# Sixteen heads: values and ones in one stationary tile, with halves exchanged by a shuffle

## What is computed

```python
def _mha(xq, xk, xv, Wq, bq, Wk, bk, Wv, bv, Wo, bo, causal):
    ...
    s = jnp.einsum('bhqe,bhke->bhqk', q, k) * (1.0 / math.sqrt(D_MODEL))
    ...
    w = jax.nn.softmax(s, axis=-1)
    o = jnp.einsum('bhqk,bhke->bhqe', w, v)
    ...
    return o @ Wo.T + bo
```

## Time and profile before

| what | us |
|---|---|
| median of 3 runs | 1870.6 |
| lowest and highest run | 1862.0, 1876.38 |
| the profiled execution | 1865.85 |
| its span (first to last instruction) | 1864.1 |
| PE busy in it | 1732.8 |
| DVE, ACT, POOL busy | 763.1, 650.5, 133.3 |

### The profile page before, as it was taken

How to read it: one execution, slowest core, us unless ns; L and a number is a source line. 1 busy time by engine, 2 the same in 40 slices (tenths; PEclk the granted TensorE clock), 3 DMA queues, 4 the chain that set the end, 5 groups by cost and what they waited for, 6 DMA issues and landing times.

```text
span 1864.1 us, 36432 instructions
## 1 busy us (share of the span) xinstructions
PE 1732.8 (93%) x16204; PEld 1128.2 (61%) x16204; DVE 763.1 (41%) x1644; ACT 650.5 (35%) x1257; POOL 133.3 (7%) x318
## 2 busy tenths in 40 slices
PE   7999989999999998999999999999899889868998
PEld 6555546656566555555567775554577666654565
DVE  1344445454553224431123332324466666652222
ACT  2343434343544343211133331225333333313333
POOL 1111010000000000000000000000011111110000
PEclk9888999999998999899999999999799999979999
DMA  3211000000000001000010000000000000001022
GB/s 136 87 42 33 17 24 2 2 2 2 2 2 2 23 0 69 1 19 1 0 69 1 2 2 23 0 1 6 23 2 2 2 2 2 2 26 42 1 60 71
DMA packets 19214, 37.45 MB, mean 20 GB/s; under 512 B 2001, under 2 KB 17137, under 8 KB 17777
## 3 DMA queue, kind: packets, MB, share of 16 engines
q1 hardware_dynamic: 19056, 35.12, 5.6%
HBM read 33.48 MB, written 1.64 MB: 19 GB/s over the span
## 4 chain that ended last, share of the span: by engine, by line
PE 85%; DVE 11%; ACT 2%; issue 1%; DMA 0%; SPq 0%; DVEq 0%; ACTq 0%
PE psum L389 37%; PE psum L525 10%; PE psum L702 9%; PE psum L434 7%; PE psum L505 7%; DVE maxima L1279 3%; PE psum L502 2%; PE psum L472 2%; DVE denoms L1306 2%; PE psum L793 2%; PE psum L821 1%; PE psum L834 1%; PE psum L790 1%; PE psum L802 1%; DVE t L1368 1%
## 5 line engine op out<-in xcount | busy, mean ns | idle before, releaser
L1279 DVE TENSOR_REDUCE maxima<-psum 100x2 f32<-100x722 f32 (+3 forms) x332 | 249.6, 761 | 240.8 <-PE psum L472 129.9
L389 PE MATMUL psum<-x_resid,weights 128*128 128x400 f32 x832 | 294.7, 504 | 3.5 <-ACT q_then_o L914 1.3
L974 ACT ACTIVATE probs<-psum 128x800 f32<-128x800 f32 (+3 forms) x240 | 179.0, 748 | 296.4 <-PE psum L505 295.6
L389 PEld LDWEIGHTS psum<-x_resid,weights 128*128 128x128 f32 x832 | 156.1, 191 | 119.5 <-issue 3.4
L702 PE MATMUL psum<-weights 128*128 128x400 f32 x512 | 175.0, 499 | 0.7 <-DVE maxima L1279 0.7
L434 PE MATMUL psum<-ctx_t,weights 128*128 128x361 f32 x384 | 148.6, 517 | 27.9 <-DVE maxima L1279 26.7
L389 PE MATMUL psum<-weights,ctx_t 128*128 128x256 f32 (+1 forms) x576 | 162.8, 409 | 0.7 <-ACT weights L914 0.7
L502 PE MATMUL psum<-max_rows,ones_bf 32*128 32x100 bf16 (+7 forms) x1152 | 137.5, 236 | 19.4 <-DVE max_rows L1290 12.7
L957 ACT ACTIVATE values<-psum 128x256 f32<-128x256 f32 (+2 forms) x176 | 67.4, 383 | 218.6 <-PE psum L389 218.5
L702 PEld LDWEIGHTS psum<-weights 128*128 128x128 f32 x512 | 97.2, 190 | 75.1 <-DVE maxima L1279 0.8
L1306 DVE RECIPROCAL denoms<-psum 128x200 f32<-128x200 f32 x65 | 91.4, 1406 | 107.5 <-PE psum L525 107.5
(11 more groups left out here) (144 smaller groups left out, 2214.8 us busy)
## 6 DMA issues: line engine op xcount, KB each, us to landing
weights<-in_w SPq DMA_DIRECT2D x2, 3072.0 KB, 10.3
staged<-in_ctx SPq DMA_DIRECT2D x32, 128.0 KB, 2.1
values<-in_ctx SPq DMA_DIRECT2D x32, 128.0 KB, 2.2
weights<-in_w SPq DMA_DIRECT2D x3, 1024.0 KB, 4.8
weights<-in_src SPq DMA_DIRECT2D x1, 2368.0 KB, 13.6
weights<-in_w SPq DMA_DIRECT2D x1, 2048.0 KB, 8.8
weights<-in_tw SPq DMA_DIRECT2D x2, 1024.0 KB, 5.1
staged<-in_ctx SPq DMA_DIRECT2D x16, 105.0 KB, 2.1
```

The lines of the kernel that those rows point to most:

```text
L389: i = nc.tensor.matmul(PS[0:rows, bk, 0:n], lhs, rhs, start=k == 0, stop=k == len(terms) - 1)
L974: nc.scalar.activation(PT[0:kn, k % PROBS_KEPT, :, 0:n], PS[0:kn, bk:bk + 2, 0:n], ACT.Exp).then_inc(act_results, mark("act", f"{t} p{b} { ...
L1279: nc.vector.reduce_max(top, src, AX).then_inc(dve_results, mark("dve", f"{t} m{b} {j}"))
```

## The change

The zeros in `values` become ones, so the stationary tile of e = 0 is [values | ones] and that of e = 1 is [ones | values]. The two products go to two places in the bank instead of being added, and the products with `ones_halves` are gone, for the stages with 16 heads only. Each of the two results has values in one half of the 32 rows and denominators in the other, so numerators and denominators have to be sorted by masks (`halves`, a column of 0 and 1 for each half) and the denominators moved by 16 rows. For this, ACT gets two instructions (`act_second`) and DVE has five where it had two. `act_second` stands in ACT's list at token P1; for the last batch it stands ahead of f0's first evacuation. The order of the tokens is the same.

```diff
--- before.py
+++ after.py
@@ -22,6 +22,7 @@
 KCH = [(0, 128), (128, 128), (256, C - 256)]
 SCH = [(0, S)]
 MASKED = -1.0e30
+SWAP = list(range(16, 32)) + list(range(16))
 
 
 FOLDS = [("sq", "sa_q_b", "m_bq"), ("sk", "sa_k_b", "m_bk"), ("sv", "sa_v_b", "m_bv"),
@@ -193,6 +194,7 @@
         PR = sb("probs", [P, PROBS_KEPT * 800])
         STG = sb("staged", [P, 2560])
         DN = sb("denoms", [P, DC, S])
+        SH = sb("second_heads", [P, 2, DC, S])
         MX = sb("maxima", [S, 2, P])
         MB = sb("max_rows", [P, 2, 4 * S], BF16)
         SC = sb("scan_state", [P, 9, DC * B])
@@ -201,7 +203,6 @@
         CO = sb("constants", [P, NCONST])
         ONEM = sb("ones_mean", [P, P])
         ONEB = sb("ones_bf", [P, P], BF16)
-        ONEH = sb("ones_halves", [P, 2, 32])
         ONES = sb("ones", [P, 64])
         IDB = sb("ident_bf", [P, P], BF16)
         NEGB = sb("neg_bf", [S, 4, S], BF16)
@@ -362,8 +363,8 @@
                 return V[0:kn, b % 2, kc, (c * 4 + i) * 64 + e * 32:(c * 4 + i) * 64 + e * 32 + 32]
             return V[0:kn, b % 2, kc, c * P + ATT[t]["tile"] * i:c * P + ATT[t]["tile"] * (i + 1)]
 
-        def ones_of(t, kn, e):
-            return ONEH[0:kn, e, :] if ATT[t]["e"] == 2 else ONES[0:kn, 0:ATT[t]["tile"]]
+        def ones_of(t, kn):
+            return ONES[0:kn, 0:ATT[t]["tile"]]
 
         def probs_of(t, b, i, c, kc, kn, e):
             a = ATT[t]
@@ -508,6 +509,7 @@
 
         def pe_values(pe, t, b, c):
 
+
             a = ATT[t]
             lastk = len(a["keys"]) - 1
             if due(f"{t} v{b} {lastk} out"):
@@ -517,13 +519,13 @@
                 pe.wait_ge(act_results, at(f"{t} p{b} {r}"))
             bk = held.take(pe, f"{t} o{b}", f"{t} on{b}") if c == 0 else book.banks[f"{t} o{b}"]
             for part in range(2):
-                o = part * DC * S + c * S
-                for e in range(a["e"]):
-                    for kc, (k0, kn) in enumerate(a["keys"]):
-                        for i in range(a["tiles"]):
-                            lhs = ones_of(t, kn, e) if part else values_of(t, b, kc, kn, i, c, e)
-                            mm = nc.tensor.matmul(PS[tile_rows(t, i), bk, o:o + S], lhs, probs_of(t, b, i, c, kc, kn, e),
-                                                  start=e == kc == 0, stop=e == a["e"] - 1 and kc == lastk)
+                e = part if a["e"] == 2 else 0
+                o = (2 * c + e) * S if a["e"] == 2 else (DC * part + c) * S
+                for kc, (k0, kn) in enumerate(a["keys"]):
+                    for i in range(a["tiles"]):
+                        lhs = values_of(t, b, kc, kn, i, c, e) if part == 0 or a["e"] == 2 else ones_of(t, kn)
+                        mm = nc.tensor.matmul(PS[tile_rows(t, i), bk, o:o + S], lhs, probs_of(t, b, i, c, kc, kn, e),
+                                              start=kc == 0, stop=kc == lastk)
             mm.then_inc(products_ready, mark("pe", f"{t} o{b} {c}"))
 
         def pe_out(pe, t, g, m, ring):
@@ -956,6 +958,18 @@
                 dst = V[0:kn, b % 2, kc, 0:D]
             nc.scalar.activation(dst, src, ACT.Copy).then_inc(act_results, mark("act", f"{use} out"))
 
+        def act_second(act, t, b):
+
+            old = earlier(t, b, 1)
+            if old:
+                if due(f"{old[0]} on{old[1]}"):
+                    act.wait_ge(dve_results, at(f"{old[0]} on{old[1]}"))
+            if due(f"{t} o{b} 1"):
+                act.wait_ge(products_ready, at(f"{t} o{b} 1"))
+            second = PS[:, bank(f"{t} o{b}"), 0:2 * DC * S].rearrange("p (c e q) -> p c e q", c=DC, e=2)[:, :, 1, :]
+            nc.scalar.activation(SH[:, 0], second, ACT.Copy, scale=const("halves", 2)[:, 0:1]).then_inc(act_results, mark("act", f"{t} sd{b}"))
+            nc.scalar.activation(SH[:, 1], second, ACT.Copy, scale=const("halves", 2)[:, 1:2]).then_inc(act_results, mark("act", f"{t} sn{b}"))
+
         def act_probs(act, t, b, r):
             a = ATT[t]
             _, of = a["rounds"][r]
@@ -1074,6 +1088,8 @@
                     for kind, n in tokens(t):
                         if kind == "R":
                             act_probs(act, t, b, n)
+                        elif kind == "P" and n == 1 and ATT[t]["e"] == 2 and (b or t == "c0"):
+                            act_second(act, *((t, b - 1) if b else ("s0", B - 1)))
                         elif kind == "V" and b + 1 < B:
                             act_vals(act, t, b + 1, n)
                         elif kind == "K" and b + 2 < B:
@@ -1088,6 +1104,8 @@
         def act_beside(act, of, g):
             parts = []
             if g == 0 and of in AFTER:
+                if ATT[AFTER[of]]["e"] == 2:
+                    act_second(act, AFTER[of], B - 1)
                 if AFTER[of] in NORM_OF:
                     parts.append(later(5, act_chain(act, NORM_OF[AFTER[of]], NG - 1)))
             elif g and of in NORM_AFTER:
@@ -1302,6 +1320,25 @@
             if old:
                 if due(f"{old[0]} on{old[1]}"):
                     dve.wait_ge(dve_results, at(f"{old[0]} on{old[1]}"))
+            if ATT[t]["e"] == 2:
+                first = PS[:, bk, 0:2 * DC * S].rearrange("p (c e q) -> p c e q", c=DC, e=2)[:, :, 0, :]
+                if due(f"{t} sn{b}"):
+                    dve.wait_ge(act_results, at(f"{t} sn{b}"))
+                dens, nums = SH[:, 0], SH[:, 1]
+                nc.vector.scalar_tensor_tensor(dens, first, const("halves", 2)[:, 1:2], dens, ALU.mult, ALU.add).then_inc(dve_results, mark("dve", f"{t} dn{b}"))
+                nc.vector.scalar_tensor_tensor(nums, first, const("halves", 2)[:, 0:1], nums, ALU.mult, ALU.add).then_inc(dve_results, mark("dve", f"{t} nu{b}"))
+                if due(f"{t} dn{b}"):
+                    dve.wait_ge(dve_results, at(f"{t} dn{b}"))
+                nc.vector.stream_shuffle(DN[:, :, :], dens, SWAP).then_inc(dve_results, mark("dve", f"{t} sw{b}"))
+                if due(f"{t} sw{b}"):
+                    dve.wait_ge(dve_results, at(f"{t} sw{b}"))
+                nc.vector.reciprocal(DN[:, :, :], DN[:, :, :]).then_inc(dve_results, mark("dve", f"{t} rc{b}"))
+                if due(f"{t} rc{b}"):
+                    dve.wait_ge(dve_results, at(f"{t} rc{b}"))
+                if due(f"{t} qm{b}"):
+                    dve.wait_ge(pool_results, at(f"{t} qm{b}"))
+                nc.vector.tensor_tensor(QO[:, b // GB % 2, :, b % GB * S:(b % GB + 1) * S], nums, DN[:, :, :], ALU.mult).then_inc(dve_results, mark("dve", f"{t} on{b}"))
+                return
             if len(parts) == 3:
                 nc.vector.reciprocal(DN[:, :, :], dens).then_inc(dve_results, mark("dve", f"{t} rc{b}"))
             elif parts[0] < 2:
@@ -1625,11 +1662,6 @@
             nc.vector.memset(EPS[:, 1:2], 1e-6).then_inc(dve_results, mark("dve", "p2"))
             nc.vector.memset(ONEB[:, :], 1.0).then_inc(dve_results, mark("dve", "p3"))
             nc.vector.memset(ONES[:, :], 1.0).then_inc(dve_results, mark("dve", "p4"))
-            nc.vector.memset(ONEH[:, :, :], 0.0).then_inc(dve_results, mark("dve", "p5"))
-            if due("p5"):
-                dve.wait_ge(dve_results, at("p5"))
-            nc.vector.memset(ONEH[:, 0, 0:16], 1.0).then_inc(dve_results, mark("dve", "p6"))
-            nc.vector.memset(ONEH[:, 1, 16:32], 1.0).then_inc(dve_results, mark("dve", "p7"))
             if due("vectors"):
                 dve.wait_ge(sems["constants_loaded"], at("vectors"))
             nc.vector.tensor_copy(IDB[:, :], IDENT).then_inc(dve_results, mark("dve", "p8"))
@@ -1717,7 +1749,7 @@
 
         def program_pool(pool):
             waited.clear()
-            nc.gpsimd.memset(V[:, :, :, :], 0.0).then_inc(pool_results, mark("pool", "v pads"))
+            nc.gpsimd.memset(V[:, :, :, :], 1.0).then_inc(pool_results, mark("pool", "v pads"))
             nc.gpsimd.memset(MX[:, :, :], 0.0).then_inc(pool_results, mark("pool", "pads"))
             if due("made"):
                 pool.wait_ge(dve_results, at("made"))
```

## The result

The changed kernel takes 1927.35 us (median of 3 runs, 1923.11 to 1928.59) against 1870.6: the ratio is 1.030 with a 95% interval of 1.024 to 1.037. Not no change, as forecast, but 57 us slower. Rival B had the right mechanism and still too small a price.

A forecast was written before the change was run, and what follows sets the result against it. PE was taken as the bound, with R2 waiting for DVE's T0 reduction in c0. From 1865.85 us, 16.1 came off and 17 were added for the clock: 1866.8, or 1871.5 on the median, put at 1868; range 1846 to 1892.

The forecast's parts named there:

- Rival B: R2 to R4 of each c0 batch: every wait brings the clock down, 42 us lost, 1892 us in all; chance 0.20.
- What bounds: In c0, R2 waits 0.39 us for T0's reduction behind the normalisation; any lengthening behind P1 is paid in full.
- What goes: The ones products leave PE: 33.2 us in c0, 10.8 in s0, some 46 with the stages' borders.
- What comes: From P1 to T0's reduction, copies, masks, shuffle and handovers lengthen the way by 1.7 us, bounds 1.3 and 2.4.
- R2 waits about 2.1 us: In c0, R2 comes 4.4 us after P1's end, waiting 2.1 us instead of 0.39; 15 batches lose 25.5 us.
- the clock falls in 10 of the 15 ... 10 x 1.7 = 17 us more: Around R2's new waits in c0, the clock falls in two of three batches, each losing 1.7 us: 17 us more.
- PE is not the only limit behind R2: Reason given for pricing each clock fall in c0 at the trace's shortest, 1.7 us, rather than 2.5.
- rows 12: Trace stretches at 90, 575 and 405 us where PE waited: the clock fell after two and held in one.
- Rival A: In c0 the waits are too short to lower the clock; 16.1 us come out, 1849.8 or 1854.5 us; chance 0.25.
- s0: Shorter products save 10.8 us in s0, less 3.0 for T1's reduction up to 0.6 us late in 5 batches: 7.8.

The follow-up runs named there:

- e4: Changed kernel with ten unused products added for PE ahead of R2 in every batch of c0, chain untouched; 1877.11 us, ratio 1.0036.
- e5: Kernel before, ones products kept, with two ACT copies, two masks and a shuffle, results unused, put ahead of its reciprocal; 1964.77 us, ratio 1.051.
- e6: Changed kernel, c0 normalisation split in DVE's list: masks and shuffle behind T0's reduction, reciprocal and multiplication behind T1's; 1828.34 us, ratio 0.978.
- e1: Changed kernel with the whole c0 normalisation moved in DVE's list behind T0's reduction, same instructions; 1840.71 us, ratio 0.983.
- e2: Kernel before, ones products kept, with only the c0 normalisation moved in DVE's list behind T0's reduction; 1854.33 us, ratio 0.9925.
- e7: Kernel before, ones products kept, with only two ACT copies, results unused, put ahead of its reciprocal; 1928.41 us, ratio 1.032.

## Why the prediction was wrong

*What bounds.* Right: R2 behind T0's reduction is the place, and lengthening behind P1 was paid in full, 15 times.

*What goes.* Right for c0: 33.2 us worked out, 31.6 measured with the chain kept short.

*What comes.* Nearly: 2.0 us instead of 1.7. From the start of the first copy to the start of the first mask are 0.87 us where the sum had 0.62: the copies are 90 ns longer each, and from ACT to DVE it takes 0.12 us instead of 0.03. The two masks took 0.70 instead of 0.80, and the 0.11 taken off for more overlap did not come. "R2 waits about 2.1 us" was 2.4.

*The step that failed* is "the clock falls in 10 of the 15 ... 10 x 1.7 = 17 us more". Each factor was too small. In the trace after, all 15 long waits have a fall; and 391.5 us at a mean of 0.81 is 74 us of full-speed time lost in 16 stretches, 4.6 us a stretch, where I took the shortest of the trace, 1.7. Measured with PE kept busy, the falls cost 49 to 53 us of time, not 17. I had the longer ones in front of me: the fall at 95 us already lost 2.5 us in its first five, and I argued it away with "PE is not the only limit behind R2". So did c0's own fall, the one of which rows 12 show the start: it lasted 10.2 us at half clock and lost 5.1.

```profile
575.80:586.00 10.20, 9.56 (x121) 6.79 (x121) 5.74 (x8) 2.73 (x5) 0.00 (x0) 0.50 0.01 2
```

That PE is not the only limit does show: the changed kernel lost 65 us more of full-speed time in c0 than `e4` and took 49.4 us longer. But that is three quarters of the price, not a third. And of the three stretches of rows 12 I weighed two falls against one that held, though PE would be idle for longer than in all three; that pointed to nearly 15.

*Rival B* had the place and the mechanism, but 2.8 us a batch; it was 3.3 to 3.5, and its tipping point (1.1 us a batch) was passed three times over. Its "against", that PE at half clock would shorten the wait, did not help: the fall begins at the wait's end, 1.1 us ahead of it at the earliest, and the clock is up again when the next one begins.

*Rival A* (the clock holds): a DVE step between dense stretches of products did cost PE its clock here, in `e5` with not one product fewer, 0.98 to 0.82. The Trainium skill (TensorE: Matmul & The Clock Gate, "Loop structure matters more than you think") says that it does not, of a loop whose next products follow immediately; this case agrees for the kernel before, with its waits of 0.4 us, and in `e5` the next products did not follow immediately but waited 2.4 us. What the Trainium skill says of another kernel (same title, "A second HAM failure mode"), that small idles between groups made the clock go up and down, is what these traces show: waits of 1.3 to 2.4 us, 10 to 15 falls.

*s0.* 7.8 us were forecast, and the working has a slip: with 1.7 us more on one side, 0.36 on the other and 1.26 of slack, T1's reduction would be 0.8 us late, not 0.6. PE's waits for reductions by DVE between 48 and 250 us grew from 5.6 to 10.7 us, where 3.0 had been taken off and 0.4 at the border. s0 up to its last product with values ends at 262.4 us before and at 257.5 after, but kernels whose s0 is the same as the changed one's end it at 261.4, 264.6 and 265.5 (`e6`, `e1`, `e4`), and one whose s0 is that of the kernel before at 264.6 (`e2`), with other falls of the clock. A gain in s0 is not shown. Nor is a loss behind c0: the 5.8 us are of the size by which that stretch differs among the kernels (1266.5 to 1272.6 us).

The sum by measured terms for c0: - 31.6 (ones) + 35 (chain: 38.5 less the 4 of the filling) + 53 (clock, from the same pair: 49.4 and the same 4) = + 56, as measured; the three terms are steps from one run to the next, so they must add up, and what they tell is how the loss divides.

## What to carry to other kernels

Before lengthening a chain between two engines, look for what stands behind it in the in-order list of the consumer, and move the next engine's dependency ahead of it: here the same instructions in another place were worth 87 to 99 us. Where PE runs at 2.4 GHz and a change adds a wait that comes back in every batch, price it with the clock: here 2.0 us more of waiting cost 6.0 us a batch (`e5`). Filling a wait with products that nobody reads is a quick test of whether the clock is the loss.

## What was not expected of the hardware

A mean wait of only 1.3 us, once a batch of 22 us, brought the clock from 0.98 to 0.88 in c0 (`e7`); with 2.4 us it was 0.81 to 0.82, and each low stretch lost 4.6 us of full speed on average. PE's useless products kept it at 0.98 (`e4`). An ACT copy of 128x200 out of PSUM with a scale per row takes 428 ns, without one 337. A shuffle of 128x200 float32 takes 374 ns, its mask load 14 ns.
